# Frequency stage of a spectral token mixer: filter products in two 64-column tiles, mixed spectra turned by VectorE

## What is computed

```python
def _stu_conv(phi, u, n):                      # n = 4096
    Vf = jnp.fft.rfft(phi, n=n, axis=0)        # 16 filters of length 2048
    Uf_p = jnp.fft.rfft(u, n=n, axis=1)
    ...
    U_plus = jnp.fft.irfft(Vf[None, :, :, None] * Uf_p[:, :, None, :], n=n, axis=1)[:, :sl]
...
    out = jnp.einsum('btkd,k,kde->bte', U_plus, s, Mpp)
    out = out + jnp.einsum('btkd,k,kde->bte', U_minus, s, Mpm)
```

## Time and profile before

| | before |
|---|---|
| median of 3 runs | 1475.58 us (1473.2 to 1476.07) |
| the profiled execution | 1476.14 us, span 1474.5 us |
| granted TensorE clock, mean of the span | 0.931 |
| norms, convolution, first step | 0 to about 597 us |
| `m_sta` | 597.8 to 634.0 us |
| 32 units and the end of the frequency stage | 634.0 to 1225.1 us |
| last part (`finish`) | 1225.1 to 1474.5 us |
| busy over the span | PE 1257.3 us, DVE 985.8, ACT 822.3, POOL 502.7 |

### The profile page before, as it was taken

How to read it: one execution, slowest core, us unless ns; L and a number is a source line. 1 busy time by engine, 2 the same in 40 slices (tenths; PEclk the granted TensorE clock), 3 DMA queues, 4 the chain that set the end, 5 groups by cost and what they waited for, 6 DMA issues and landing times. The chain is left out here.

```text
span 1474.5 us, 37538 instructions
## 1 busy us (share of the span) xinstructions
PE 1257.3 (85%) x15089; PEld 887.7 (60%) x15089; DVE 985.8 (67%) x1420; ACT 822.3 (56%) x1487; POOL 502.7 (34%) x441
## 2 busy tenths in 40 slices
PE   1899999999999965988899999999999954965657
PEld 1455555555555532278799899899989932433334
DVE  5288888888888888765577677667767732532234
ACT  1787877888787742554466565556655521322223
POOL 2145566665566665101222223232222231000000
PEclk9999999999999986589999999999999986988778
DMA  7024455455455365328999889888889868978883
GB/s 222 1 88 145 153 190 180 145 155 184 152 180 193 106 150 172 126 82 237 271 285 289 259 255 277 240 243 267 259 255 260 250 185 314 408 309 341 332 327 131
DMA packets 179624, 317.66 MB, mean 215 GB/s; under 512 B 14805, under 2 KB 154423, under 8 KB 162935
## 3 DMA queue, kind: packets, MB, share of 16 engines
q1 hardware_dynamic: 164966, 257.47, 56.4%
q0 software_dynamic: 14592, 59.26, 11.1%
HBM read 162.93 MB, written 153.76 MB: 215 GB/s over the span
## 5 line engine op out<-in xcount | busy, mean ns | idle before, releaser
L1020 POOL DMA_DIRECT2D w_scratch<-wf x256 | 151.3, 595 | 467.5 <-ACT y_sb L1198 432.4
L1079 PE MATMUL ring<-v_mov,m_sta 105*128 105x128 f16 x4096 | 234.0, 219 | 0.0
L1079 PEld LDWEIGHTS ring<-v_mov,m_sta 105*128 105x128 f16 x4096 | 231.5, 98 | 0.4
L1215 DVE COPY hf<-ring 128x512 f32<-128x512 f32 x256 | 168.7, 689 | 26.8 <-PE ring L1079 25.8
L1198 ACT ACTIVATE hf<-ring 128x512 f32<-128x512 f32 x256 | 153.0, 598 | 58.7 <-PE ring L1079 56.7
L491 POOL TENSOR_TENSOR u_t<-u_t,root 98x1024 f32<-98x1024 f32 x62 | 118.1, 1936 | 169.7 <-DVE root L799 169.7
L535 PE MATMUL ring_norm<-x_all,center 128*128 128x448 f32 (+2 forms) x384 | 148.8, 513 | 25.0 <-PEq L211 15.7
L1404 ACT ACTIVATE out_sb<-p_turn 128x392 f32<-128x392 f32 x128 | 62.6, 498 | 189.2 <-PE p_turn L1360 174.6
L1348 PE MATMUL p_out<-w_in,last_masked 128*98 128x512 f32 x256 | 140.0, 631 | 23.9 <-DMA w_in<-w_scratch 23.9
L1393 DVE TENSOR_TENSOR x_in<-p_out,x_in 98x512 f32<-98x512 f32 x96 | 65.3, 690 | 123.0 <-DMA x_in<-x_scratch 70.0
L594 PE MATMUL ring_norm<-u_t,step_masked 98*128 98x512 f32 x256 | 126.8, 624 | 22.0 <-POOL u_t L491 22.0
(11 more groups left out here) (133 smaller groups left out, 1958.3 us busy)
## 6 DMA issues: line engine op xcount, KB each, us to landing
z_in<-z_scratch SPq DMA_DIRECT2D x32, 1076.5 KB, 8.4
z_scratch<-z_sb SPq DMA_DIRECT2D x16, 2048.0 KB, 8.9
y_scratch<-y_sb SPq DMA_DIRECT2D x32, 1024.0 KB, 9.0
yt<-y_scratch SPq DMA_DIRECT2D x64, 512.0 KB, 6.3
w_scratch<-wf POOLq DMA_DIRECT2D x256, 128.0 KB, 5.3
w_in<-w_scratch SPq DMA_DIRECT2D x8, 4096.0 KB, 16.2
x_all<-in_x SPq DMA_DIRECT2D x16, 1568.0 KB, 7.6
x_scratch<-x_t SPq DMA_DIRECT2D x16, 1568.0 KB
```

The costliest lines, as they stand in the source:

```text
L1020: nc.gpsimd.dma_start(w_units[u, h, s, c], wf[64 * c:64 * c + 64, 2 * h + s].rearrange("p (g n) -> p g n", n=256)).then_inc(w_stored, 16)
L1079: mm = nc.tensor.matmul(bank[:, 2 * NF * i:2 * NF * i + 2 * NF], m_sta[:, 2 * e + 1 - n:2 * e + 3 - n, :].rearrange("k b d -> k (b d)"), v ...
L1215: return nc.vector.tensor_copy(dst, src)
```

## The change

- h: `m_sta` holds no zeros. The real and the imaginary half of a bank are two products with 64 stationary columns each, in the column tiles at 0 and 64 of the array, with nothing added. As many matmuls as before.
- mix writes its four banks so that each group of 32 partitions holds 16 neighbouring frequencies, and when all four banks are there VectorE turns them in 32x32 blocks straight from PSUM into a single `yt`: 4 instructions of 128x512 a unit. The 4 copies to `y_sb`, the store to DRAM and the two loads back are gone, with `y_sb` and its semaphores.
- inv is done one unit later, not two (`LAG_INV` = 1), with 64 rows and 64 columns a tile: 8 matmuls for 16. Its moving operand takes every 32nd element of `yt`.
- The owner of a copy is no longer its place: all turns are VectorE's, h chunks 1, 3, 5, 8, 10, 12, 14 VectorE's and the other 9 ScalarE's; x and inv are shared half and half as before.
- `m_sta`'s chunks are written with 8 neighbouring f16 in the inner loop (before, every 128th element), and GpSimd's memset of it goes.

```diff
-    inv = inv.transpose(0, 1, 4, 2, 3, 5).reshape(NUNIT, 2 * NALPHA, 128)
-    inv = np.concatenate([inv, inv], 1)
+    inv = inv.transpose(0, 1, 4, 2, 3, 5).reshape(NUNIT, 4, 16, 2, 2 * NA)
+    inv = inv.transpose(0, 1, 3, 2, 4).reshape(NUNIT, 128, 2 * NA)
...
-LAG_INV = 2
+LAG_INV = 1
 RING = 7
+
+H_ON_VECTOR = (1, 3, 5, 8, 10, 12, 14)
+
+
+def owner(stage, k):
+
+    if stage == "mix":
+        return 1
+    return int(k in H_ON_VECTOR) if stage == "h" else k % 2
...
-        y_sb = [sb(f"y_sb{i}", [128, NF // 4, 2 * CH]) for i in range(2)]
-        yt = [sb(f"yt{i}", [128, NIMG // 2, 2, CH]) for i in range(2)]
+        yt = sb("yt", [128, CH, NIMG])
...
-        m_sta = sb("m_sta", [STACK, 2 * CH + 1, CH], F16)
+        m_sta = sb("m_sta", [STACK, CH, CH], F16)
...
             def body(u, slot, use):
 
+                sp.wait_ge(chunk_ready, chunks_until(u, pos["x", 3]))
+                after_wait(sp, sp_turn)
                 if not known(u, NUNIT - 2, NUNIT - 1):
-                    sp.wait_ge(chunk_ready, chunks_until(u, pos["x", 3]))
-                    after_wait(sp, sp_turn)
                     load(u + 2, slot)
-                for e in range(2):
-                    sp.wait_ge(saved[e], chunks_until(u, pos["mix", 3], e))
-                after_wait(sp, sp_turn)
-                store_y(slot)
                 if not known(u, 0, 1):
                     load_inv(u, slot)
-                sp.wait_ge(y_stored[slot], 16 * use)
-                after_wait(sp, sp_turn)
-                load_y(slot)
...
+            stage, k, _ = chunks[at]
+            last = pos["mix", 3] if stage == "mix" else at
+            eng.wait_ge(saved[owner(stage, k)], chunks_until(w, last, owner(stage, k)))
...
                                 mm = nc.tensor.matmul(
-                                    bank[:, 2 * NF * i:2 * NF * i + 2 * NF],
-                                    m_sta[:, 2 * e + 1 - n:2 * e + 3 - n, :].rearrange("k b d -> k (b d)"),
-                                    v_mov[:, NF * (1 - n):NF * (3 - n)], start=(n == 0), stop=(n == 1))
+                                    bank[CH * n:CH * n + CH, 2 * NF * i:2 * NF * i + 2 * NF], m_sta[:, e, :],
+                                    v_mov[:, NF * (1 - n):NF * (3 - n)], start=True, stop=True,
+                                    tile_position=(0, CH * n))
...
-                                f = 16 * k + 4 * i + j
+                                f = 16 * j + 4 * k + i
...
+                        for h in range(2):
+                            for c, row in ((0, 0), (1, 1), (1, 0), (0, 1)):
+                                images = slice(16 * h + 8 * c, 16 * h + 8 * c + 8)
+                                rows = slice(64 * row, 64 * row + 64)
+                                mm = nc.tensor.matmul(
+                                    ring[64 * c:64 * c + 64, pos["inv", 2 * h + row] % RING, :],
+                                    inv[1 - slot][rows, :], yt[rows].rearrange("p e i -> p i e")[:, images, :],
+                                    start=True, stop=True, tile_position=(64 * row, 64 * c))
...
-            return (m_sta[:, 1:2 * CH + 1, DCH * c:DCH * c + DCH].rearrange("k (e t) d -> k d e t", t=2)[:, :, :, 0],
-                    ring[0:STACK, c % RING, :].rearrange("k (d e) -> k d e", e=CH))
+            return (m_sta[:, :, DCH * c:DCH * c + DCH],
+                    ring[0:STACK, c % RING, :].rearrange("k (d e) -> k e d", e=CH))
...
                     elif stage == "mix":
-                        copy(y_sb[slot][:, 4 * k:4 * k + 4, :].rearrange("p i n -> p (i n)"), bank
-                             ).then_inc(saved[which], 1)
+                        e = slice(16 * k, 16 * k + 16)
+                        nc.vector.transpose(
+                            yt[:, e, :], ring[:, first_mix:first_mix + 4, :]
+                            .rearrange("p b (i r e) -> p e r (b i)", r=2, e=CH)[:, e]).then_inc(saved[which], 1)
```

More of the change, by code:

```diff
@@ L896, in chunks_until @@
     plan = unit_chunks()
+    mine = [(stage, at) for stage, k, at in plan if engine in (None, owner(stage, k))]
     if isinstance(u, int):
[L898 to L902, removed]
+        return sum(1 for w in range(u + 1) for stage, at in mine
+                   if chunk_is_there(stage, w) and (w < u or at <= p))
+    missing = LAG_INV * sum(1 for stage, at in mine if stage in TAIL)
+    return len(mine) * u - missing + sum(1 for stage, at in mine if at <= p)
 def mix_frequencies(nc, d, keep):
@@ L909, in mix_frequencies @@
     NCH = len(chunks)
-    assert NCH % RING == 0 and NCH % 2 == 0
+    assert NCH % RING == 0
     pos = {(s, k): p for s, k, p in chunks}
+    first_mix = pos["mix", 0] % RING
+    assert first_mix + 4 <= RING
     with ExitStack() as own:
@@ L1026, in _ @@
             pool.sem_inc(w_free, 1)
-            nc.gpsimd.memset(m_sta[:].rearrange("k e n -> k (e n)").bitcast(F32), 0.0).then_inc(m_zeroed, 1)
             store(0)
@@ L1037, in bank_free @@
                 w, at = (u, p - RING) if p >= RING else (u - 1, p - RING + NCH)
[L1038 to L1042, removed]
+            else:
+                before = [(w, at) for w in range(u + 1) for stage, _, at in chunks
+                          if chunk_is_there(stage, w) and at % RING == p % RING and (w < u or at < p)]
+                if not before:
+                    return
                 w, at = before[-1]
-                eng.wait_ge(saved[at % 2], chunks_until(w, at, at % 2))
+            stage, k, _ = chunks[at]
+            last = pos["mix", 3] if stage == "mix" else at
+            eng.wait_ge(saved[owner(stage, k)], chunks_until(w, last, owner(stage, k)))
         def all_saved(eng, u, p):
@@ L1099, in unit @@
                             bank_free(pe, u, pos["inv", at])
[L1100 to L1104, removed]
-                                    rows = slice(32 * n, 32 * n + 32)
-                                    mm = nc.tensor.matmul(
-                                        ring[64 * c:64 * c + 64, pos["inv", n] % RING, :], inv[slot][rows, r, :],
-                                        yt[slot][rows, 8 * c:8 * c + 8, r, :], start=(r == 0), stop=(r == 1),
-                                        tile_position=(32 * n, 64 * c))
-                                    if c and r:
-                                        mm.then_inc(chunk_ready, 1)
+                        pe.wait_ge(saved[1], chunks_until(u - 1, pos["mix", 3], 1))
+                        pe.wait_ge(inv_loaded[1 - slot], 16 * (use if slot else use - 1))
+                        after_wait(pe, pe_turn)
+                        for h in range(2):
[6 more added lines that the diff above has]
+                                    start=True, stop=True, tile_position=(64 * row, 64 * c))
+                                if c != row:
+                                    mm.then_inc(chunk_ready, 1)
                     if stage != "inv":
@@ L1115, in body @@
             def body(u, slot, use):
-                unit(u, slot, use, True, not known(u, 0, 1))
+                unit(u, slot, use, True, not known(u, 0))
             for c in range(M_CHUNKS):
@@ L1156, in unit @@
                 for stage, k, p in chunks:
[L1157 removed]
+                    if owner(stage, k) != which or not (tail if stage in TAIL else head):
                         continue
[L1159 removed]
+                    eng.wait_ge(chunk_ready, chunks_until(u, pos["mix", 3] if stage == "mix" else p))
                     bank = ring[:, p % RING, :]
                     if (stage, k) == ("inv", first_inv):
[L1162 to L1164 removed]
+                        eng.wait_ge(w_free, u)
                     if stage == "x":
@@ L1207, in _ @@
             unit = saver(act, 0, copy)
-            two_by_two(act, NUNIT, lambda u, slot, use: unit(u, slot, use, True, not known(u, 0, 1)))
-            for u in (NUNIT, NUNIT + 1):
-                unit(u, u % 2, u // 2 + 1, False, True)
+            two_by_two(act, NUNIT, lambda u, slot, use: unit(u, slot, use, True, not known(u, 0)))
+            unit(NUNIT, NUNIT % 2, NUNIT // 2 + 1, False, True)
         @block.vector
@@ L1246, in _ @@
             unit = saver(dve, 1, copy)
-            two_by_two(dve, NUNIT, lambda u, slot, use: unit(u, slot, use, True, not known(u, 0, 1)))
-            for u in (NUNIT, NUNIT + 1):
-                unit(u, u % 2, u // 2 + 1, False, True)
+            two_by_two(dve, NUNIT, lambda u, slot, use: unit(u, slot, use, True, not known(u, 0)))
+            unit(NUNIT, NUNIT % 2, NUNIT // 2 + 1, False, True)
 def finish(nc, d, keep):
```

32 lines of the change are left out of this document (7 added, 25 removed).

## The result

The changed kernel takes 1483.32 us (median of 20 runs, 1473.96 to 1490.07) where the kernel before takes 1475.25 (20 runs, 1469.17 to 1480.12). The ratio is 1.0052, with an interval of 1.0035 to 1.0069: slightly slower, by 8 us, where 24 us less were forecast. The 1483 still lies inside the forecast's range of 1430 to 1490, but for a cause that the range was not drawn for. The profiled execution of the changed kernel took 1476.21 us with a span of 1474.4; it is one of the quicker ones, 7 us under the median, while the profiled execution of before lies 0.9 above its own.

What follows compares the result with a forecast made beforehand. PE alone bounded the unit before; afterwards PE and VectorE take turns. Savings of 3.9 (start), 1.4 (first unit), 7.5 (later units) and 11.5 us (end), together 24.3, gave 1451.8, so a median of 1451 us; range 1430 to 1490.

Steps and rivals of the forecast that it cites:

- I take no loss: inv: the moving operand's 128-byte step was taken to cost nothing, inv staying 1.93 us; at most 0.57 us more a unit.
- held-up units: Frequency stage, units waiting while DMA engines are shared: 15 us lost for 20.6 before, with 6 and 25 as ends.
- the turns: VectorE's four block turns a unit from PSUM: 0.69 us each like a copy, 2.76 us for four.
- Rival 3: inv: the strided moving operand costs 0.57 us more a unit, 18 us more in all, 1469 us; chance 6%.
- What lies on the path: After mix, VectorE's turns, v_mov, x and h copies delay inv to 11.13 us; unit 16.69 us for 16.79.
- Rival 1: VectorE's turns are dear: at 1.0 us each 38 us more, 1490; at twice a copy 1537; chance 13%.
- h: h matmuls in two side-by-side column tiles: 0.29 us a chunk of 8, h without waits 3.6 to 4.7 us for 7.25.
- Rival 2: h gains nothing, through slow weight loads in column tiles or tiles not overlapping: 25 us more, 1476; chance 8%.
- Start and end: `m_sta` copies 3.9 us less, first unit 1.4 less; last mix to next part's load 20.6 us for 32.1, 11.5 less.
- rival 4: PE's gaps lower its clock: x at the lower level for half its time, 56 us more, 1507; chance 5%.

## Why the prediction was wrong

**The step that failed** is the one on inv, in the prediction's words "I take no loss", with an upper bound of 0.57 us a unit. Measured were 1.64 us a unit (3.57 for 1.93), 31 x 1.64 = 51 us over the stage, and that is all of the miss and more: in the profiled executions 24 us are missing, the 51 of inv less 12 for a chain that was shorter than forecast, 9 for fewer held-up units and 6 in the other pieces. Without these other errors the result would have been near 1500, outside the range; its end at 1490 had been drawn for dear turns. The bound came from a stationary operand of f32 with a step, put at 1.08 ns a column (taken over all 8 loads, its 0.90 us give 1.15, and a bound of about 0.7). The rows of the changed kernel show 0.86 us for 512 moving columns, 1.68 ns each: a stationary operand's row doesn't bound a moving operand. The moving columns at no loss take 0.84 ns each (0.43 us a pass). The prediction had no row of a moving operand with a step, so its rows gave this term no upper end, and 0.57 should not have stood as one. It looked for an error in the turns and the held-up units first; neither was what failed. Rival 3 had the mechanism and a third of its price (18 us), at 6%.

The page of the Trainium skill that was weighed there, "SBUF — State Buffer", section Door 1: The DMA port swizzle, was right where the row was followed against it. The runs agree with its rule of 16-byte lines: the loss is there at every step tried that puts each element in a new line (4, 8 and 32 elements), and nearly absent at 8 bytes (0.45 for 0.43 us a pass). The page gives the penalty no size. These runs give a factor of 2 in a pass at the full clock, no more at 128 bytes than at 16, and none at the lower clock.

**What lies on the path** was right: VectorE's chain from the turns to the h copies sets inv's start. It came at 10.75 us for 11.13, mostly since turns run 0.61 us apart back to back where 0.69 was taken. The extra turn (+0.60 to 0.64 a unit) and the moved copies (-0.98) show the chain as the path. Rival 1 (dear turns) is out: the mean of one is 685 ns in the profile's groups.

**h** was right: two column tiles overlap. 48 matmuls take 1.65 us, 34 ns each, and their 48 loads 1.49 us, 31 ns each, less than the 37 ns of the earlier trace rows. By the pages of the Trainium skill that the prediction weighed, "TensorEngine Tiling (Array Packing)", section Restrictions, and "TensorE: Matmul & The Clock Gate", section LDWEIGHTS, it would be 53 ns. The rows refute that price for these loads; whether Fast Weight Load is off in them no row shows. Rival 2 is out.

**Held-up units** cost 5.8 us, not 15 (ends 6 and 25). That fits the trip of `y_sb` that is gone, and longer units with more slack. With shorter units the same loads cost more: over units 1 to 4, 3.3 us where a unit takes 18.63, 6.0 at 18.56 (the extra turn), 5.5 at 17.96, 8.0 at 16.26 and 11.7 at 15.28, which the split of the loads recovered. So the stall goes, roughly, with the unit's length, which the sum did not have; what the missing trip alone gives was not measured.

**Start and end.** The `m_sta` copies shrank from 2.54 and 2.72 us to 0.69 and 0.75 (with the zeros still between the columns too, in the run with h as before), the stage by 3.67 for 3.9; the first unit by 1.75 for 1.4; the end is 17.8 us for 20.6, because the first copy to `wf` at 1212.6, 7.1 after the start of the stores before it (1205.54), found them landed, and the forecast had taken 11.3 for that from the earlier trace rows.

**The clock** (rival 4, 5%) shows in short stretches of single units. Two windows of the changed kernel, columns as in the earlier trace rows:

```profile
962.00:964.00 2.00, 1.07 (x32) 0.91 (x32) 1.96 (x4) 1.15 (x3) 0.00 (x0) 1.00 0.85 357
964.00:966.00 2.00, 2.00 (x46) 1.88 (x42) 2.00 (x5) 1.52 (x4) 0.00 (x0) 0.60 0.54 195
```

Behind a stretch in which PE is busy for 1.07 of 2 us (h, waiting for VectorE) the granted clock falls to a mean of 0.60 in the next 2 us, so for most of them to the lower level of 1.2 GHz (0.50). Most units have the same stretch and keep the full clock, as the window of 84 us at 1.00 shows, so the stretch alone does not bring the fall. That unit takes 18.01 us (955.99 to 974.00), 0.05 more than others, so in the middle it is almost hidden: h waits for VectorE anyway, and the strided inv is no slower at the lower clock. The rival as worked out, 56 us, is out for the profiled execution. Whether such stretches make the 7 us between it and the median, whose runs have no traces, stays open; the mean clocks of the 20 runs (0.931 to 0.937) go with their times only loosely, and 8 us slower against -0.1 in the profiles is not explained further.

## What to carry to other kernels

When a change makes TensorE read its moving operand with a step, price it at double (at the full clock) until a row of a moving operand says otherwise, and look whether runs of 32 bytes can be read instead and the order put right in the copy out of PSUM, whose time here stayed at 0.69 us. When work moves to an engine in whose program the next unit's first steps stand behind it, add up that engine's chain between the two hand-overs, then give part of it to the other engine; here that was worth 0.98 us a unit. And time the two halves of a change apart: here one was worth 42 us and hid behind the other.

## What the runs showed of the hardware

- A moving f32 operand of 512 columns in 64x64 tiles: 0.43 us a pass contiguous or in runs of 32 bytes, 0.45 with a step of 8 bytes, about double with steps of 16, 32 and 128 bytes (0.86 measured at 128), all at the full clock. At a granted clock of 0.50 a pass takes 0.86 us both contiguous and with a step of 128 bytes.
- VectorE turns 128x512 f32 from PSUM in 32x32 blocks in 685 ns (mean of one), one per 0.61 us back to back, the price of a copy.
- A 2-byte output of 105x512 written in steps of 256 bytes takes 2.54 us on ScalarE and 2.72 on VectorE; in runs of 16 bytes it takes 0.69 and 0.75.
- Weight loads of 64 f16 columns in column tiles come every 31 ns.
